# Edge scores of a graph attention layer: one PSUM pair for each expansion, and the product of the magnitudes on VectorE alone

## What is computed

```python
hr_src, hr_dst = h_r[:, src], h_r[:, dst]
diff = hr_dst - hr_src
score = s_src + s_dst + sum(diff * a_dif) + sum(abs(diff) * a_abs) \
        + sum(hr_src * hr_dst * a_prd)
```

## Time and profile before

| | us |
|---|---|
| median of 3 runs | 3604.73 (3603.67 to 3625.55) |
| the profiled execution | 3586.76 |
| its span | 3584.8 |
| first and last difference of the score stage (L1073) start at | 564.7 and 1893.4 |

### The profile page before, as it was taken

The page is one execution under the profiler, slowest core; times in us unless marked ns, Lnnn a source line. Parts: engine busy times, 40 slices in busy tenths (PEclk is TensorE's granted clock), DMA queues, the critical chain, the costliest instruction groups (busy, mean ns, idle before and its releaser), DMA issues. The chain is left out here.

```text
span 3584.8 us, 65271 instructions
## 1 busy us (share of the span) xinstructions
PE 2740.9 (76%) x17311; PEld 1764.0 (49%) x17312; DVE 2248.0 (63%) x4027; ACT 1448.0 (40%) x2941; POOL 1651.8 (46%) x1562
## 2 busy tenths in 40 slices
PE   2599887989999989989991057777777777779892
PEld 2366544666666666666661034444444444477440
DVE  3667635777777777777772967777777777742111
ACT  1233315888888888888882010000000000033220
POOL 1133204444444444444440047777777777612112
PEclk9799988999999999999996579999999999959996
DMA  3012134555555555555555035666666665641124
GB/s 115 18 61 63 56 110 124 143 142 144 142 142 144 143 142 144 143 142 144 143 136 157 0 101 165 173 175 172 174 174 174 173 174 174 164 138 48 62 77 134
DMA packets 181565, 461.62 MB, mean 129 GB/s; under 512 B 50534, under 2 KB 66338, under 8 KB 180739
## 3 DMA queue, kind: packets, MB, share of 16 engines
q0 software_dynamic: 116400, 372.54, 37.2%
q1 hardware_dynamic: 55105, 83.86, 7.5%
q10 hardware_dynamic: 10002, 4.53, 0.5%
HBM read 413.88 MB, written 46.86 MB: 129 GB/s over the span
## 5 line engine op out<-in xcount | busy, mean ns | idle before, releaser
L1313 POOL DMA_INDIRECT rows_e<-message_rows,edge_dst x672 | 809.8, 1205 | 431.6 <-ACTq L1286 222.9
L1047 POOL DMA_INDIRECT rows_v<-target_rows,edge_dst x672 | 639.0, 951 | 684.0 <-DVE w L1073 577.1
L1355 PE MATMUL ps_sum<-messages,node_onehot 128*125 128x512 f32 x1344 | 745.9, 643 | 243.6 <-DVE messages L1331 154.9
L1073 DVE TENSOR_TENSOR w<-rows_v,ps_u 128x520 f32<-128x520 f32 x672 | 468.0, 696 | 376.1 <-issue 284.4
L1164 ACT ACTIVATE slope<-w_abs,a_abs,minus_prd 128x256 f32<-128x256 f32 x1344 | 697.8, 593 | 0.1
L1111 PE MATMUL ps_u<-edge_space,source_onehot_t 125*128 x4032 | 593.6, 280 | 133.5 <-DVE w L1073 131.0
L1331 DVE TENSOR_TENSOR messages<-rows_e,edge_space 128x1024 f32<-128x1024 f32 x336 | 411.6, 1225 | 246.9 <-DMA rows_e<-message_rows,edge_dst 246.5
L1111 PEld LDWEIGHTS ps_u<-edge_space,source_onehot_t 125*128 125x128 bf16 x4032 | 362.9, 97 | 357.8 <-issue 279.0
L1356 PEld LDWEIGHTS ps_den<-edge_space,node_onehot 128*125 128x125 f32 x1344 | 254.5, 189 | 329.3 <-issue 329.3
L1678 ACT COPY gate_t<-ps_count 128x32 f32<-128x32 f32 x1 | 0.2, 186 | 1030.6 <-PE ps_count L1611 1030.6
L1086 DVE TENSOR_TENSOR slope<-w_abs,slope 128x1024 f32<-128x1024 f32 x336 | 409.4, 1218 | 4.2 <-ACT slope L1164 4.2
(11 more groups left out here) (380 smaller groups left out, 2943.9 us busy)
## 6 DMA issues: line engine op xcount, KB each, us to landing
scores<-score SPq DMA_DIRECT2D x1344, 8.0 KB
edge_space<-in_L_ffn_w_dram SPq DMA_DIRECT2D x24, 512.0 KB, 4.7
rows_v<-target_rows,edge_dst POOLq DMA_INDIRECT x672
rows_e<-message_rows,edge_dst POOLq DMA_INDIRECT x672
source_parts<-edge_space SPq DMA_DIRECT2D x20, 380.9 KB
edge_space<-source_parts SPq DMA_DIRECT2D x4, 1904.3 KB
token_rows_out<-token_y SPq DMA_DIRECT2D x27, 256.0 KB, 2.7
edge_space<-scores SPq DMA_DIRECT2D x2, 2688.0 KB, 28.2
```

Source lines behind the costliest of these rows:

```text
L1047: nc.gpsimd.indirect_dma_start(rows[q][:, j, :], None, tab_v, bass.IndirectOffsetOnAxis(ap=edge["dst"][:, tile:tile + 1], axis=0)).then_in ...
L1073: v.tensor_tensor(w[q][:, j, :].rearrange("p (a b) -> p a b", a=2), rows[q][:, j, :].rearrange("p (a b) -> p a b", a=2), ps_u[:, :, 0:HALF ...
L1313: nc.gpsimd.indirect_dma_start(rows[q][:, j, :], None, tab_e, bass.IndirectOffsetOnAxis(ap=edge["dst"][:, tile:tile + 1], axis=0)).then_in ...
L1355: nc.tensor.matmul(ps_sum[h][:, :], onehot[h][:, j, :], messages[h][:, j, :], start=j == 0, stop=j == GROUP - 1)
```

## The change

- `ps_u` becomes two pairs of banks, one for each tile j of a group. The expansion of tile j of group n waits for the difference of the same tile of group n - 1, no longer for the difference just before it.
- `ps_w` becomes one pair of banks instead of two. The transposes of group n wait for the magnitudes of group n - 1.
- The slopes go: ScalarE's list loses its four operations a group. VectorE computes z = (d - corner) * d in four operations `scalar_tensor_tensor` of 256 columns, one per set of 128 dimensions, where corner = 2 * a_abs / a_prd is a value per partition. The factor -a_prd / 2 moves into the weights of `add_heads`, which now has its own 128 x 32 weights for each set of dimensions (`head_weight`).
- The lists of VectorE and TensorE change their order: the two differences stand side by side, and so do the two expansions.
- The setup computes corner and `head_weight`, with |a_prd| raised to at least 1e-15: seven more chained small operations on 128 x 4, and four on 128 x 32.

```diff
+        z = sbs("z", [P, KF, GE])
-        ps_w = [ps(f"ps_w{h}", [P, KF, GE]) for h in range(2)]
-        ps_u, ps_onehot = ps("ps_u", [P, 2, 512]), ps("ps_onehot", [L, GROUP, P], BF16)
+        ps_w, ps_onehot = ps("ps_w", [P, KF, GE]), ps("ps_onehot", [L, GROUP, P], BF16)
+        ps_u = [ps(f"ps_u{j}", [P, 2, 512]) for j in range(GROUP)]
...
-            link(v.tensor_scalar(minus_prd[:, :], minus_prd[:, :], -0.5, None, ALU.mult))
-            dve.sem_inc(vectors_set, 2)
+            link(v.scalar_tensor_tensor(corner[:, :], prd[:, :], -1.0, prd[:, :], ALU.mult, ALU.max))
+            link(v.tensor_scalar(tiny[:, :], corner[:, :], SMALLEST, None, ALU.is_lt))
+            link(v.tensor_scalar(corner[:, :], corner[:, :], SMALLEST, None, ALU.is_ge))
+            link(v.tensor_tensor(prd[:, :], prd[:, :], corner[:, :], ALU.mult))
+            link(v.scalar_tensor_tensor(prd[:, :], tiny[:, :], SMALLEST, prd[:, :], ALU.mult, ALU.add))
+            link(v.reciprocal(corner[:, :], prd[:, :]))
+            link(v.scalar_tensor_tensor(corner[:, :], corner[:, :], 2.0, a_abs[:, :], ALU.mult, ALU.mult))
+            link(v.tensor_scalar(minus_prd[:, :], prd[:, :], -0.5, None, ALU.mult))
+            for c in range(KF):
+                ins = v.tensor_scalar(head_weight[:, c, :], head_sum[:, :], minus_prd[:, c:c + 1], None, ALU.mult)
+            link(ins)
+            dve.sem_inc(vectors_set, 1)
...
-                                ps_u[:, :, 0:HALF], ALU.subtract).then_inc(differed, 1)
+                                ps_u[j][:, :, 0:HALF], ALU.subtract).then_inc(differed, 1)
...
-                at_least(dve, slope_set, n + 1)
+                at_least(dve, abs_set, n + 1)
                 at_least(dve, summed, n - BUFS + 1)
-                v.tensor_tensor(slope[h][:, :, :], w_abs[h][:, :, :], slope[h][:, :, :], ALU.mult).then_inc(z_set, 1)
-
-            in_turns(v, TURNS, ((2, differ_first), (5, multiply), (2, differ_second), (0, locate)), TURN)
+                for c in range(KF):
+                    ins = v.scalar_tensor_tensor(z[h][:, c, :], w_abs[h][:, c, :], corner[:, c:c + 1], w_abs[h][:, c, :], ALU.subtract, ALU.mult)
+                ins.then_inc(z_set, 1)
+
+            in_turns(v, TURNS, ((2, differ_first), (2, differ_second), (5, multiply), (0, locate)), TURN)
...
-                at_least(pe, differed, n * GROUP + j)
+                at_least(pe, differed, n * GROUP + j - 1)
...
-                        ins = nc.tensor.matmul(ps_u[:, half, 0:HALF], onehot_t[q % BUFS][:, j, :], rows_of_part, start=part == 0, stop=part == PARTS - 1)
+                        ins = nc.tensor.matmul(ps_u[j][:, half, 0:HALF], onehot_t[q % BUFS][:, j, :], rows_of_part, start=part == 0, stop=part == PARTS - 1)
...
-                at_least(pe, abs_set, n - 1)
+                at_least(pe, abs_set, n)
...
-                    ins = nc.tensor.matmul(strip, head_sum[:, :], slope[h][:, c, :], start=True, stop=True)
+                    ins = nc.tensor.matmul(strip, head_weight[:, c, :], z[h][:, c, :], start=True, stop=True)
...
-            in_turns(nc.tensor, TURNS, ((2, expand_first), (1, turn_onehot), (6, add_heads), (2, expand_second), (3, transpose)), TURN)
+            in_turns(nc.tensor, TURNS, ((2, expand_first), (2, expand_second), (1, turn_onehot), (6, add_heads), (3, transpose)), TURN)
...
-            in_turns(sc, TURNS, ((4, magnitudes), (1, keep_onehot), (4, slopes), (6, keep_scores)), TURN)
+            in_turns(sc, TURNS, ((4, magnitudes), (1, keep_onehot), (6, keep_scores)), TURN)
```

More of the change, by code:

```diff
@@ L50 @@
 BIG = 1e38
+SMALLEST = 1e-15
 def linker(eng, sem, base=0):
@@ L999, in score_edges @@
         w, w_abs = [sb(f"w{q}", [P, GROUP, EW]) for q in range(TURN)], sbs("w_abs", [P, KF, GE])
-        slope = sbs("slope", [P, KF, GE])
+        z = sbs("z", [P, KF, GE])
         score = sbs("score", [P, GE])
-        a_abs, minus_prd = sb("a_abs", [P, KF]), sb("minus_prd", [P, KF])
+        a_abs, prd, minus_prd = sb("a_abs", [P, KF]), sb("prd", [P, KF]), sb("minus_prd", [P, KF])
+        tiny, corner = sb("tiny", [P, KF]), sb("corner", [P, KF])
         head_i, head_f = sb("head_i", [P, 1], I32), sb("head_f", [P, 1])
-        head_sum = sb("head_sum", [P, STRIP])
-        ps_w = [ps(f"ps_w{h}", [P, KF, GE]) for h in range(2)]
-        ps_u, ps_onehot = ps("ps_u", [P, 2, 512]), ps("ps_onehot", [L, GROUP, P], BF16)
+        head_sum, head_weight = sb("head_sum", [P, STRIP]), sb("head_weight", [P, KF, STRIP])
+        ps_w, ps_onehot = ps("ps_w", [P, KF, GE]), ps("ps_onehot", [L, GROUP, P], BF16)
+        ps_u = [ps(f"ps_u{j}", [P, 2, 512]) for j in range(GROUP)]
         ps_heads = ps("ps_heads", [P, 2, GE])
         onehot_set, onehot_turned, onehot_kept = sem("onehot_set"), sem("onehot_turned"), sem("onehot_kept")
-        expanded, turned, abs_set, slope_set = sem("expanded"), sem("w_turned"), sem("abs_set"), sem("slope_set")
+        expanded, turned, abs_set = sem("expanded"), sem("w_turned"), sem("abs_set")
         z_set, summed = sem("z_set"), sem("summed")
@@ L1022, in _ @@
         def _(sp):
-            for tile, part in ((a_abs, 3), (minus_prd, 4)):
+            for tile, part in ((a_abs, 3), (prd, 4)):
                 for h in range(HEADS):
@@ L1122, in transpose @@
                 at_least(pe, differed, n * GROUP + GROUP)
-                at_least(pe, abs_set, n - 1)
+                at_least(pe, abs_set, n)
                 for c in range(KF):
                     for j in range(GROUP):
-                        ins = nc.tensor.transpose(ps_w[q % 2][:, c, j * P:(j + 1) * P], w[q][:, j, c * P:(c + 1) * P], ident[:, :])
+                        ins = nc.tensor.transpose(ps_w[:, c, j * P:(j + 1) * P], w[q][:, j, c * P:(c + 1) * P], ident[:, :])
                 ins.then_inc(turned, 1)
@@ L1145, in _ @@
             sc = nc.scalar
-            act.wait_ge(vectors_set, 2)
             def keep_onehot(n, q, turn):
@@ L1156, in magnitudes @@
                 at_least(act, z_set, n - BUFS + 1)
[L1157 to L1165, removed]
+                sc.activation(w_abs[h][:, :, :], ps_w[:, :, :], ACT.Abs).then_inc(abs_set, 1)
             def keep_scores(n, q, turn):
```

## The result

The changed kernel takes 3564.99 us (3560.47 to 3572.74, 4 runs) beside 3613.85 (3603.67 to 3625.55) of the kernel before, a ratio of 0.987 [0.982, 0.991]. The forecast was 3356, with a range of 3295 to 3440. So a gain of 1.3% came where 7% was expected. The profiled execution took 3572.74, its span 3570.8.

A forecast was written before the change was run, and what follows sets the result against it. ScalarE and the VectorE-TensorE loop on `ps_u` bound the score stage; a period of 3.2 for 3.94 us saves 248 over 335 groups, setup +2, end -2: 3586.8 - 248 = 3339, times 1.005 = 3356 us, range 3295 to 3440.

The forecast's parts named there:

- The two loops: Score stage: ScalarE's 3.82 us and the VectorE-TensorE turns on `ps_u`, 4.13, hold the period; both must go.
- It holds, with a slack of 0.2 us: Score stage, new order: the path from `locate` to the difference fits beside one VectorE iteration of 2.91, so TensorE runs through.
- about 0.2 for semaphores: Handover allowance added to 2.5 us of turn, heads, transposes and expansion between `locate` and the difference.
- the slower engine sets the period: Score stage: with handovers fitting, TensorE's 3.09 to 3.24 us against VectorE's 2.91 decides; 3.2 taken.
- The prediction's own signs of being wrong: Score stage: a period above 3.5 us, or over 0.3 us a group of waits left between VectorE and TensorE.
- Rival 4: Score stage: an unseen wait, the 0.40 ahead of the second difference, keeps the period near 3.9, 3600 us; chance 0.03.
- TensorE's own work: Score stage: TensorE's time a group if it never waits, 3.09 to 3.24 us, some small gaps being the sequencer's.
- Rival 1: VectorE's four products don't overlap: 0.422 each, VectorE 3.24, period 3.32, median 3396 us; chance 0.10.
- DMA: Score stage: same bytes in a shorter time, 176 GB/s, at the edge of the message stage's 171.
- Rival 2: Score stage: POOL's gathers or the DMA engines become the bound, period 3.45, median 3440 us; chance 0.20.
- Setup and tail: Outside the loop: added setup operations cost 2 us, the stage's end without last slopes saves 2.

The follow-up runs named there:

- p1: Kernel before with two `ps_u`, one `ps_w` and the new orders, slopes still on ScalarE: 3421.03 us against 3487.11, period 3.46.
- p2: Kernel before with slopes gone and four products on VectorE, its buffers and orders kept: 3636.49 us against 3487.11, period 4.08.
- a0: Changed kernel run again unedited, late signals present: 3503.78 us against 3595.43 of the kernel before, ratio 0.976, period 3.68.
- j1: Changed kernel with the transposes' completion signalled by a later TensorE instruction, no work added: 3567.13 us against 3485.43 of the kernel before, period 3.92.
- a1: Changed kernel unedited, third comparison, prompt signals: 3347.21 us against 3481.14 of the kernel before, ratio 0.961, period 3.24.
- e4: Changed kernel with one 1024-column product, corner left out (wrong scores), instead of four: 3346.85 us, kernel before 3491.20, period 3.24.
- b0: Kernel before run again unedited, late signals present: 3593.74 us beside 3595.43, period 3.94.

## Why the prediction was wrong

- **The two loops.** Their mechanism is confirmed, by p1 and p2 above all. Their lengths weren't. The prediction took the 4.13 of the earlier trace rows as what handovers on one `ps_u` cost; where signals are prompt the loop has 3.60, and ScalarE's own work is 3.42 (297.06 of 300 at 3.46), not 3.82, since its neighbours overlap; the earlier trace rows had 3.51 already (267.20 of 300 at 3.94), with 0.43 to spare. So of the 0.74 us that should go, 0.41 (3.65 - 3.24) were the loops' and some 0.3 (3.95 - 3.65) were lateness that the change doesn't touch.
- **The step that failed** is "It holds, with a slack of 0.2 us" with "about 0.2 for semaphores", and with it "the slower engine sets the period". It sets the time of a handover by the end of TensorE's work in the trace. In the measured place the signal came up to 2.4 us behind. The changed kernel has one `ps_w`, so that the next transposes wait for magnitudes that a late signal holds up, and its differences wait for expansions that end close before them; little slack is left in these loops to take up a late signal. The term of the sum that failed is the period, 3.20 for a measured 3.87. The prediction's own signs of being wrong both came: a period above 3.5, and 0.70 us a group of VectorE's waits for TensorE where 0.3 was the limit. Measured against the same kernel with prompt signals, late ones cost the kernel before 0.30 us a group (3.95 against 3.65) and the changed one 0.63 (3.87 against 3.24), in a0 0.44. Hence 0.41 of gain becomes 0.08, or 0.25 in the comparison of a0. That lateness is enough to do this is shown by j1, where one signal a group that comes 1.6 us late costs 0.68; that it is the whole of it isn't, since nothing here takes it away in the same place. That the operations last the same in both speaks for it.
- **Rival 4** named the right row, the 0.40 ahead of the second difference for an expansion "long past", with 0.03, and left it as a wait that I couldn't see. It was in the open: in the kernel before VectorE waits so ahead of 125 of 152 second differences, 0.25 us in the mean (31.3 us in all), for expansions long past.
- **TensorE's own work** was read at 3.09 to 3.24, and the sum took 3.2. In a1 the steps are 0.93 + 1.34 + 0.21 + 0.45 + 0.32 = 3.25. The upper end holds; nothing of the gaps was the sequencer's to give back.
- **VectorE**: predicted 2.91, upper bound 3.24. The four products take 1.59 to the next start and not 1.36: each lasts 0.479, not 0.422, and the next starts 0.40 behind it, not 0.34. With 0.38 and 1.28 for the rest it is 3.25, equal to TensorE's. Rival 1 had the right sum by the wrong way: they do overlap, by 0.08, and each is longer. It costs nothing while TensorE needs 3.24 (e4).
- **POOL** was to be held up for 1.36 to 1.69 by the four products, its median "above 0.95 in any case". The gather at 1203.76 of a1 lies wholly within the products and takes 0.95; of the 370 gathers between 1000 and 1600 us there 366 start during a product, and none of them takes more than 0.96:

```profile
L1049 POOL DMA_INDIRECT rows_v<-target_rows,edge_dst x672: 940/946/1204, 552.7 to 1636.8; - x168
```

  In e4, with one `tensor_tensor` instead, it does wait, in each of the 185 gathers that start during a product (median 1.69):

```profile
1205.95 1.22 DVE L1098 TENSOR_TENSOR z<-w_abs 128x1024 f32<-128x1024 f32 x1
...
1206.31 1.69 POOL L1049 DMA_INDIRECT rows_v<-target_rows,edge_dst  x1 [0.31 <-DVE w L1085]
```

  It ends 0.83 behind the product, as in the earlier trace rows. So what the earlier trace rows show holds for that operation and not for the four; the order of the stage alone doesn't decide it. Whether it is the kind of operation or its length (256 columns for 1024) isn't shown. By the Trainium skill, "SBUF — State Buffer", section "SBUF: two separate sides", any operation of VectorE with two SBUF inputs locks out an operation of POOL that reads SBUF; the measurement differs for these `scalar_tensor_tensor`.
- **DMA**: 176 GB/s predicted, 174 in a1. Rival 2 didn't come. Setup and tail: nothing that can be read.
- **ScalarE**: 1.74 predicted, 163.72 / 92.6 = 1.77 measured.

Where signals are prompt the changed kernel takes 3347 to 3351, within 0.3% of the number; the number was made for a place in which they aren't, so that is no hit. The gain there is 3.9% (a1) and not 7%, because the kernel before is faster there as well. Rows of the kernel before showed the lateness, and I summed over it.

**Open**: what makes TensorE's signals late. It comes and goes between chips or moments with one and the same program, and holds for both kernels. The record gives chip 4 for a0 and b0, with late signals, and for j1, some 40 minutes later, with prompt ones; whether the number means the same chip it doesn't say. Nearly all late signals fall in the score stage, but not all: at the start of the message stage the kernel before has seven at 2167 to 2195 us, 0.1 to 3.2 us late, with a wait of VectorE of 2.08. It isn't the gathers' traffic as such, since the message stage gathers at 173 GB/s (2200 to 2500 us) in the same execution with prompt signals, and it begins at 569 us, ahead of the first store of scores at 587 (kernel before). Whether it needs the gathers together with TensorE's traffic wasn't seen, because no run without them is known to have met late signals. In the late traces part of the updates of VectorE and ScalarE have no record either (710 of 1027 and 486 of 772 are there in the first, against 1229 of 1232 and 924 of 924 in a1); whether that has the same cause isn't known. Nor is it known whether the matmuls' results or only their signals are late.

## What to carry to other kernels

When an engine is idle behind work that ended long before by the trace, add up these gaps before costing a loop: they are part of the period, and a change of buffers doesn't take them away. A tighter handover removes the loop's slack as well as its length, so ask what a signal that is 1 us late would do in the new order, with j1's edit if in doubt. And if two loops hold a stage, half the change can be worse than none (p2); run the halves in one comparison with the kernel before, whose own time tells whether the comparison is like the last.

## What the runs showed of the hardware

- Completion signals of TensorE come 13 to 25 ns behind the modelled end in one place (a1) and up to 2.4 us behind it in another (the first trace), same program and stage, with clock 1.00 in both from 1000 to 1300 us.
- `scalar_tensor_tensor` over 256 columns with a per-partition pointer takes 0.479 us (a1) and the next starts 0.40 behind. One without the pointer takes 0.422; behind a `tensor_tensor` of 256 columns the next operation starts 0.34 after it.
- Four of these, each with the same SBUF tensor at both inputs, leave POOL's indirect gather at 0.95 us (a1); one `tensor_tensor` of 1024 columns makes it 1.69 (e4).
